# Probabilities times v with v stationary: two heads in two column halves, row sums divided out by a transposed bank, k projection moved up

## The reference, cut to what matters

```
h = shift_token(x);  q, k, v = split(h @ wqkv)          # 8 heads of 64
q, k = rotary_xpos(l2norm(q) * qs, l2norm(k) * ksc)
# window w attends to windows w-1 and w, at most 128 tokens back
attn = softmax(where(mask, -max, einsum(bq * 8, bk)))
out  = einsum('bhwij,bhwjd->bhwid', attn, bv)           # <- what the change touches
x = x + out @ wo                                        # <- and this
h = layernorm(shift_token(x)) * lg + lb
a, g = split(h @ w1 + b1);  x = x + (a * gelu(g)) @ w2 + b2
```

## Time and profile before

| | value |
|---|---|
| three runs, us | 4843.39, 4847.38, 4853.73 |
| profiled execution: first to last instruction, us | 4843.6 |
| TensorE matmul busy | 4406.7 us, 91% |
| VectorE busy | 3426.7 us, 71% |
| ScalarE busy | 2548.9 us, 53% |
| GpSimd busy | 2690.2 us, 56% |
| mean granted TensorE clock | 0.974 of full speed |

### The profile page before, as it was taken

One profiled execution on the slowest core, in us unless ns is written; L12 is line 12 of the kernel. 1 busy time (PEld: TensorE's weight loads), 2 busy tenths in 40 slices (PEclk: granted clock), 3 DMA queues, 4 the chain that ended last, 5 costly groups with the idle time before them and its releaser, 6 DMA issues.

```text
span 4843.6 us, 98674 instructions
## 1 busy us (share of the span) xinstructions
PE 4406.7 (91%) x36902; PEld 3602.1 (74%) x36992; DVE 3426.7 (71%) x5743; ACT 2548.9 (53%) x5920; POOL 2690.2 (56%) x1654
## 2 busy tenths in 40 slices
PE   5888888888888886999999999999999999999998
PEld 3666565666666654888888888888888888888887
DVE  3888888888888884666666666666666666666665
ACT  2433333333343323666666666666666666666664
POOL 4999999999999993333333333333333333333332
PEclk8999999999999997999999999999999999999999
DMA  4344333333343401000000000000000000000000
GB/s 77 52 57 55 52 45 46 49 45 46 45 57 50 57 12 54 11 17 15 15 20 13 15 20 13 15 20 24 15 25 20 19 26 17 22 20 24 21 19 25
DMA packets 128879, 151.18 MB, mean 31 GB/s; under 512 B 16959, under 2 KB 94614, under 8 KB 128406
## 3 DMA queue, kind: packets, MB, share of 16 engines
q1 hardware_dynamic: 128406, 144.63, 17.2%
HBM read 43.93 MB, written 25.17 MB: 14 GB/s over the span
## 4 chain that ended last, share of the span: by engine, by line
PE 38%; issue 9%; DVE 8%; ACT 3%; POOL 3%; SPq 0%; DMA 0%; DVEq 0%; POOLq 0%; ACTq 0%
PE b_X L1280 8%; PE b_M L1325 7%; PE b_F L1351 6%; PE b_M L1403 4%; PE b_F L1430 3%; PE b_S L1305 3%; PE b_S L1314 2%; ACT b_p L1039 2%; PE b_S L1296 1%; PE b_M L1394 1%; DVE b_hn L1138 1%; POOL b_rn L871 1%; PE b_X L1262 1%; DVE b_ss L1065 1%; DVE b_mx L1086 1%
## 5 line engine op out<-in xcount | busy, mean ns | idle before, releaser
L277 ACT ACTIVATE a_p<-a_S 128x512 f32<-128x512 f32 x1024 | 528.8, 602 | 1115.4 <-PE a_S L500 1115.4
L317 DVE TENSOR_REDUCE a_nm<-a_S 128x128 fp32r<-128x2048 f32 x256 | 584.8, 2285 | 181.6 <-PE a_S L459 178.3
L1039 ACT ACTIVATE b_p<-b_S,b_nb,b_rn 128x256 f32<-128x256 f32 (+1 forms) x1024 | 537.4, 534 | 223.4 <-DVE b_nb L1089 222.6
L1280 PE MATMUL b_X<-b_wqkv,b_hT 128*128 128x512 f32 x2304 | 650.8, 418 | 1.5 <-DVE b_hT L1113 1.3
L221 POOL TENSOR_TENSOR a_p<-a_p,a_zi 128x512 f32<-128x512 f32 x256 | 616.4, 2408 | 62.4 <-DVE a_zi L324 62.3
L213 POOL TENSOR_TENSOR a_z<-a_p 128x1024 f32<-128x1024 f32 x256 | 605.6, 2366 | 68.6 <-ACT a_p L277 68.6
L1351 PE MATMUL b_F<-b_hnT,b_w 128*114 128x256 f32 (+1 forms) x4608 | 628.1, 285 | 5.7 <-issue 5.7
L864 POOL TENSOR_TENSOR b_t<-b_t 128x512 f32<-128x512 f32 x128 | 165.7, 1295 | 823.5 <-DVE b_t L1063 823.5
L1351 PEld LDWEIGHTS b_F<-b_hnT,b_w 128*114 128x114 f32 (+1 forms) x4608 | 572.8, 177 | 19.4 <-issue 5.9
L327 DVE TENSOR_TENSOR a_p<-a_p,a_zi 128x1536 f32<-128x1536 f32 x256 | 541.8, 2116 | 8.8
L1098 DVE TENSOR_SCALAR b_a<-b_F,w_b 114x256 f32<-114x256 f32 (+1 forms) x384 | 183.8, 479 | 427.9 <-ACT b_g L960 427.9
(11 more groups left out here) (135 smaller groups left out, 8894.7 us busy)
## 6 DMA issues: line engine op xcount, KB each, us to landing
a_q<-a_parts SPq DMA_DIRECT2D x128, 256.0 KB, 9.9
a_k<-a_parts SPq DMA_DIRECT2D x128, 256.0 KB, 10.7
a_x<-in_x SPq DMA_DIRECT2D x16, 512.0 KB, 4.1
x_after_heads<-a_n SPq DMA_DIRECT2D x64, 128.0 KB, 1.7
b_x<-x_after_heads SPq DMA_DIRECT2D x16, 512.0 KB, 3.9
x_after_layer<-b_xo SPq DMA_DIRECT2D x32, 256.0 KB, 2.3
b_x<-x_after_layer SPq DMA_DIRECT2D x16, 512.0 KB, 3.9
b_x<-x_after_heads SPq DMA_DIRECT2D x32, 256.0 KB, 2.8
```

What stands on the lines that cost most here:

```text
L277: nc.scalar.activation(probs[u % NE][:, hs], S[:, hs], ACT.Exp, scale=HDIM ** -0.5).then_inc(s_exp, 1)
L317: nc.vector.tensor_reduce(out=negmax[u % 2][:], in_=S[:].rearrange("p h q -> p q h"), axis=AX.X, op=ALU.max, negate=True).then_inc(s_nm, 1)
L1039: last = nc.scalar.activation(probs[hf][:, i, keys(w_)], SB[:, i, keys(w_)], ACT.Exp, bias=nb[hf][:, i:i + 1], scale=rn[w_ % 2][:, h:h + 1 ...
L1280: last = nc.tensor.matmul(X[i][:], hT_of(k, a), wqkv[:, b, k, i * INNER:(i + 1) * INNER], start=(k == 0 and (a, b) == PART_PAIRS[0]), stop ...
```

## The change

It has three parts, all in `layers`.

1. `times_v`: before, the transposed probabilities `PT` (128 keys x 128 queries) were stationary and v (64 columns of one head) moved, one matmul for each head and key window, giving tokens x channels in `M`. Now v of one head (128 keys x 64) is stationary and `PT` moves with 128 columns. The result is channels x tokens, already transposed. Two heads of a pair lie in the two column halves of the array (`tile_position=(0, 64 * e)`) and write the two partition halves of the same 128 columns of `M`. The number of matmuls stays.
2. The row sums now have to be applied along the moving axis. VectorE takes the reciprocals at the top of the next pass. GpSimd widens the 8 values of a token to 512 (`rwide`, which is the second half of `sq`, product with a column of ones). ScalarE copies the unnormalised output from `M` to `oU`. TensorE transposes `rwide` into `M` (four transposes, as many as before). VectorE multiplies `M` by `oU` into `oT`. The old product `o_n` on VectorE and the old copy `oT` on ScalarE are gone.
3. The k projection is issued directly behind the q projection, ahead of the output projection.

```diff
@@ -646,8 +647,10 @@
     probs = [sb(f"p{i}", [P, 4, 2 * P]) for i in range(2)]
     rs = [sb(f"rs{i}", [P, LHEADS]) for i in range(2)]
     rinv = sb("rinv", [P, LHEADS])
+
+    rwide = sq[:, 1].rearrange("p h d -> p (h d)")
     PT = [sb(f"PT{i}", [P, 4, 2 * P]) for i in range(2)]
-    o_n = sb("o_n", [P, INNER])
+    oU = sb("oU", [P, IH, P])
     oT = sb("oT", [P, IH, P])
     hs = sb("hs", [P, TILES, P])
     stats = sb("stats", [P, 2, 6])
@@ -699,9 +702,10 @@
     s_PTe = sem("PT_evacuated")
     s_AV = sem("av")
     s_ri = sem("row_sums_inverted")
-    s_on = sem("o_normalised")
-    s_oT = sem("oT")
-    s_oTe = sem("oT_evacuated")
+    s_rw = sem("inverses_widened")
+    s_oU = sem("oU_evacuated")
+    s_R = sem("inverse_sums_spread")
+    s_oTn = sem("oT_normalised")
     s_wo = sem("o_projected")
     s_x2 = sem("x2")
     s_sh = [sem(f"shifted{i}") for i in range(TILES)]
@@ -870,13 +874,20 @@
             need(pool, s_pr, 2 * t - 2)
             nc.gpsimd.tensor_tensor(rn[p][:], ssc[:], half[:], ALU.pow).then_inc(s_rn, 1)
+        def spread_inverses(t):
+            pool.wait_ge(s_ri, t + 1)
+            need(pool, s_R, t)
+            nc.gpsimd.tensor_tensor(sq[:, 1], rinv[:].unsqueeze(2).to_broadcast([P, LHEADS, LDIM]),
+                                    one_col[:].unsqueeze(2).to_broadcast([P, LHEADS, LDIM]), ALU.mult).then_inc(s_rw, 1)
+
         nc.gpsimd.memset(zero_col[:], 0.0).then_inc(s_c, 1)
+        nc.gpsimd.memset(one_col[:], 1.0).then_inc(s_c, 1)
...
-        pool.wait_ge(s_c, 8)
+        pool.wait_ge(s_c, 9)
             nc.gpsimd.affine_select(out=mask[i][:, i], in_=mask[i][:, i], compare_op=ALU.is_ge, fill=MASKED, base=0,
@@ -889,6 +900,8 @@
         def one(n, par, r, layer):
             for w_ in range(TILES):
                 T = TILES * n + w_
+                if tile_exists(T - 1):
+                    spread_inverses(T - 1)
                 if tile_exists(T - 2):
                     slot = (w_ - 2) % TILES
                     cols = slice(slot * P, (slot + 1) * P)
...
@@ -993,8 +1006,8 @@
                 if tile_exists(T + 1) or tile_exists(T - 2):
                     evacuate_hT(T, n, w_, layer)
                 if tile_exists(T - 1):
-                    act.wait_ge(s_oT, T)
-                    nc.scalar.activation(oT[:], M[:], ACT.Copy).then_inc(s_oTe, 1)
+                    act.wait_ge(s_AV, T)
+                    nc.scalar.activation(oU[:], M[:].rearrange("p (b q) -> p b q", q=P), ACT.Copy).then_inc(s_oU, 1)
                 if live:
                     exps(T, w_, 0)
                 if tile_exists(T + 1):
...
@@ -1130,6 +1143,10 @@
                 T = TILES * n + w_
                 p = w_ % 2
                 live, feed = tile_exists(T), seq_exists(n - 1)
+                if tile_exists(T - 1):
+                    dve.wait_ge(s_pr, 2 * T)
+                    need(dve, s_rw, T - 1)
+                    nc.vector.reciprocal(rinv[:], rs[1 - p][:]).then_inc(s_ri, 1)
                 if tile_exists(T - 2):
                     n2, w2_ = back(n, w_, 2)
                     p2 = par if w_ >= 2 else 1 - par
@@ -1145,18 +1162,14 @@
                     low_qkT(T, 1, p)
                 if feed:
                     value(T, 0, w_, layer)
-                if tile_exists(T - 1):
-                    dve.wait_ge(s_AV, T)
-                    nc.vector.reciprocal(rinv[:], rs[1 - p][:]).then_inc(s_ri, 1)
-                    dve.wait_ge(s_ri, T)
-                    nc.vector.tensor_tensor(o_n[:].rearrange("p (h d) -> p h d", d=LDIM),
-                                            M[:].rearrange("p (h d) -> p h d", d=LDIM),
-                                            rinv[:].unsqueeze(2).to_broadcast([P, LHEADS, LDIM]), ALU.mult
-                                            ).then_inc(s_on, 1)
                 if tile_exists(T + 1):
                     low_hT(T, w_)
                 if live:
                     row_max(T, w_, 0)
+                if tile_exists(T - 1):
+                    dve.wait_ge(s_R, T)
+                    nc.vector.tensor_tensor(oT[:], M[:].rearrange("p (b q) -> p b q", q=P), oU[:], ALU.mult
+                                            ).then_inc(s_oTn, 1)
                 if tile_exists(T - 1):
                     n1, w1_ = back(n, w_, 1)
                     p1 = par if w_ >= 1 else 1 - par
@@ -1317,14 +1330,16 @@
         def times_v(t, w_, hf):
             pe.wait_ge(s_PTe, 2 * t + hf + 1)
             slots = 1 if w_ == 0 else 2
-            for e in range(2):
-                for ps in range(2):
-                    i, h = 2 * e + ps, 4 * hf + 2 * ps + e
-                    for a in range(slots):
-                        first = hf == 0 and i == 0 and a == 0
-                        last = nc.tensor.matmul(M[:, h * LDIM:(h + 1) * LDIM], PT[hf][:, i, a * P:(a + 1) * P],
-                                                v[:, w_ if a == w_ % 2 else w_ - 1, h * LDIM:(h + 1) * LDIM], start=first,
-                                                stop=(hf == 1 and i == 3 and a == slots - 1), skip_group_check=True)
+            for ps in range(2):
+                b = 2 * hf + ps
+                for a in range(slots):
+                    for e in range(2):
+                        rows, h = slice(64 * e, 64 * e + 64), 2 * b + e
+                        last = nc.tensor.matmul(M[rows, b * P:(b + 1) * P],
+                                                v[:, w_ if a == w_ % 2 else w_ - 1, h * LDIM:(h + 1) * LDIM],
+                                                PT[hf][:, 2 * e + ps, a * P:(a + 1) * P],
+                                                start=(b == 0 and a == 0), stop=(b == IH - 1 and a == slots - 1),
+                                                tile_position=(0, 64 * e), skip_group_check=True)
             if hf == 1:
                 last.then_inc(s_AV, 1)
...
@@ -1389,21 +1404,21 @@
                 if live:
                     scores(T, w_, 0)
                 if tile_exists(T - 1):
-                    pe.wait_ge(s_on, T)
+                    pe.wait_ge(s_rw, T)
+                    pe.wait_ge(s_oU, T)
                     for b in range(IH):
-                        last = nc.tensor.transpose(M[:, b * P:(b + 1) * P], o_n[:, b * P:(b + 1) * P], ident[:])
-                    last.then_inc(s_oT, 1)
+                        last = nc.tensor.transpose(M[:, b * P:(b + 1) * P], rwide[:, b * P:(b + 1) * P], ident[:])
+                    last.then_inc(s_R, 1)
                 if tile_exists(T + 1):
                     projection_ready(T + 1, layer(0 if w_ < 3 else 1))
                     project(0, s_q)
+                    project(1, s_k)
                 if tile_exists(T - 1):
-                    pe.wait_ge(s_oTe, T)
+                    pe.wait_ge(s_oTn, T)
                     wo = W[layer(0 if w_ >= 1 else -1)]["o"]
                     for b in range(IH):
                         last = nc.tensor.matmul(M[:, 0:CH], oT[:, b], wo[:, b], start=(b == 0), stop=(b == IH - 1))
                     last.then_inc(s_wo, 1)
-                if tile_exists(T + 1):
-                    project(1, s_k)
                 if live:
                     transpose_probs(T, w_, 0)
                 if feed:
```

More of the change, by code:

```diff
@@ L627, in layers @@
     zero_col = sb("zero_col", [P, 1])
+    one_col = sb("one_col", [P, 1])
     carrier = sb("carrier", [P, 1])
@@ L974, in _ @@
         act.wait_ge(s_w, WEIGHTS)
-        act.wait_ge(s_c, 12)
+        act.wait_ge(s_c, 13)
         evacuate_hT(-1, -1, 3, lambda d: 0)
@@ L1357, in _ @@
         pe.wait_ge(s_w, WEIGHTS)
-        pe.wait_ge(s_c, 12)
+        pe.wait_ge(s_c, 13)
         tile_parity["next"] = 0
```

2 lines of the change are left out of this document (1 added, 1 removed).

## The result

| | before | after |
|---|---|---|
| median, us (four runs each, same chip) | 4848.99 | 4909.02 |
| range of the runs, us | 4843.39 to 4853.73 | 4906.43 to 4914.73 |
| ratio, 95% interval | | 1.0125 [1.0111, 1.014] |
| profiled span, us | 4843.6 | 4907.5 |
| mean granted clock | 0.974 | 0.963 |

The account below looks back on a forecast made before the run. TensorE sets the pace in one stretch, a ScalarE, VectorE and GpSimd chain in the other. 4843.6 - 71 + 44 + 3 = 4819.6 us from the profiled span; forecast 4822 us on the runs' scale, range 4768 to 4888.

Parts of the forecast that it names:

- the last sentence on GpSimd's widening: Widening beside VectorE's `hn`: no cost in odd passes; about 0.1 us of wait in even ones, 0.16 a sequence.
- the stretch C: Even pass's first probability transposes to next odd pass's `hn`; ScalarE, VectorE, GpSimd chain ends last; grows 44 us (layer 1), 3 (layer 0).
- widening runs long: Rival: GpSimd's widening takes 2.78 us beside `hn` in even passes, delaying it 1.48; 4917 us, chance 0.13.
- The clock: TensorE's granted clock should stay at full speed, as the new gaps are under 2.5 us.
- P: Odd pass's `hn` transposes to next even pass's first probability transposes; TensorE sets the pace; saves 2.23 us a sequence, 71 us.
- symptom of the k projection: In layer 1, TensorE waits 1.5 to 2.2 us for `gated` at the second feed-forward matmul.
- the even passes: `hn` there has 2.0 us of slack, nearly used up; about 0.1 us of wait, 0.16 a sequence.
- The bursts: TensorE's matmuls of probabilities times v: 1.06 us for a full burst of 16 records, 0.63 for a half one.
- dear case: Rival: each array layout change costs 0.276 us at both burst ends; 32 us more, 4854 us, chance 0.10.
- only TensorE's work: Rival: all shorter bursts count in full, as TensorE is 91% busy; saves 150 us, 4697 us, chance 0.05.
- hidden lateness: Rival: exponentials wait for their table load anyway, so 47 us from VectorE's lateness vanish; 4775 us, chance 0.15.
- no overlap: Rival: the column halves do not run side by side, bursts stay at 1.73 us; about 4893 us, chance 0.07.

Follow-up runs that it names:

- e4: Kernel before, plus one unused GpSimd product of the size and at the place of the widening: 4974.84 us, ratio 1.0259.
- e1: Changed kernel, with GpSimd's widening waiting until both halves of `hn` are written: 4814.47 us, ratio 0.9934.
- e3: Changed kernel, with the widening waiting for `hn` and the k projection back behind the output projection: 4795.95 us, ratio 0.9898.
- e5: Kernel before, with only the k projection moved up: 4890.33 us, ratio 1.0081.
- e8: Changed kernel, with the widening waiting for `hn` in odd passes only: 4817.41 us, ratio 0.9925.

## Why the prediction was wrong, step by step

**The step that failed** is the last sentence on GpSimd's widening: "In odd passes `gated` is already in front; the reciprocal fits into VectorE's idle 0.22 before `hn`: nothing." It priced the collision in the passes with 2.0 us of slack and called it nothing in the passes without any. That `gated` is in front does not protect `hn`. It holds only the first half, and the widening is next in GpSimd's queue, so it starts as the second half does. The rows for it were there: `gated` ends at 3007.34 + 0.45 = 3007.79, the second half of `hn` runs from 3007.39 to 3007.88, and whatever GpSimd does next holds it. By the forecast's own rule (`hn` ends with the product) and its 1.3 us the second half would have ended 0.1 behind 3007.79 + 1.30, at 3009.19 instead of 3007.88: 1.3 us in 64 odd passes, 84 us. With the measured 1.04 the delay is 1.00, 64 us. The experiments show the same: e4 adds 1.98 and 1.99 us a sequence to the stretch C, and e1 takes 1.99 and 1.82 away. The rival "widening runs long" had the right mechanism in the wrong passes, with the wrong cause: the product is short (1.04).

**The clock**, "should stay at full speed, as the new gaps are under 2.5 us", failed too. Waits for `hn` of 2.0 us in layer 1, and two of some 1.5 us in layer 0, were followed by stretches at half clock that the waits of at most 1.2 us before had not brought. Both steps are undone in e1, which is 95 us faster than the changed kernel by the medians and 101 by the profiled spans. In the table, times 16, 61 us of that lie in the stretch C, which is the collision, and 40 in P. The half-clock stretches behind `hn` explain 33 of the 40 (1.9 us a sequence in layer 1, 0.2 in layer 0); the last 7 stay open.

**Right:** what is left when the failed steps are undone, in its sum and in its parts. e1 is 36 us faster where 25 were foreseen. P shrank by 2.35 us a sequence in layer 0 and 2.25 in layer 1, foreseen 2.23. The stretch C moved by -0.07 and +2.61, foreseen +0.16 and +2.74. The 2.23 was worked out with VectorE's product hidden behind q and k, so it holds for e1 only: in e3, where q stands alone ahead of the output projection, P shrank by 1.49 and 1.44. The symptom of the k projection at the second feed-forward matmul and its size in the kernel before (e5) came out as well, and so did the even passes (e8). There the forecast's own terms give more than it wrote: 2.0 of slack less 1.27 less 0.95 is a wait of 0.2 us, not 0.1.

**The bursts** were foreseen at 1.06 and 0.63 and measured at 1.02 and 0.58. Eight records more cost 0.44 us, 55 ns each, as the forecast had for the loads (54 ns), and 0.14 us is left for both ends. Ahead of a first burst the two transposes also take longer, 0.36 us (3020.75 to 3021.11) instead of 0.27 (3007.94 to 3008.21). The Trainium skill, TensorEngine Tiling (Array Packing), section Key Properties, says that changing the tiling mode drains TensorE. The trace agrees, at about 0.1 us a change, and the dear case of 0.276 at each end is out. The waits for `oU` were 0.40 and 0.52 in tiles 0 and 1 against 0.40 and 0.60.

**The rivals** "only TensorE's work", "hidden lateness" and "no overlap" are excluded by the waits, by e5 and by the bursts.
